# Edge feature projections moved from the attention stage into stage one

## The reference

```python
q = (xn @ Wq + bq).reshape(n, H, DH)     # n = 2500, H = 8 heads, DH = 32
k = (xn @ Wk + bk).reshape(n, H, DH)
v = (xn @ Wv + bv).reshape(n, H, DH)
ep = ef @ We + be                        # ef: 40000 x 64, We: 64 x 32
scores = jnp.einsum('ehd,ehd->eh', q[dst], k[src] + ep[:, None, :]) * scale
scores = scores * ew[:, None]
m = segment_max(scores, dst); ex = jnp.exp(scores - m[dst])
attn = ex / segment_sum(ex, dst)[dst]
out = segment_sum(attn[:, :, None] * v[src], dst) @ Wo + bo
```

## Time and profile before

| | us |
|---|---|
| median of 3 runs (1723.24 to 1728.3) | 1725.58 |
| span of the profiled execution, first to last instruction | 1668.6 |
| median above that span | 57.0 |
| PE busy with matmuls | 1495.7 |
| DVE busy | 1028.6 |
| POOL busy | 781.2 |
| ACT busy | 615.6 |

### The profile page before, as it was taken

One profiled execution on the slowest core, in us unless ns is written; L12 is line 12 of the kernel. 1 busy time (PEld: TensorE's weight loads), 2 busy tenths in 40 slices (PEclk: granted clock), 3 DMA queues, 4 the chain that ended last, 5 costly groups with the idle time before them and its releaser, 6 DMA issues. The chain is left out here.

```text
span 1668.6 us, 23723 instructions
## 1 busy us (share of the span) xinstructions
PE 1495.7 (90%) x6795; PEld 1005.9 (60%) x6795; DVE 1028.6 (62%) x2542; ACT 615.6 (37%) x1534; POOL 781.2 (47%) x738
## 2 busy tenths in 40 slices
PE   4999788999999999998356799999999999999996
PEld 2554314665666777777233467767766767767785
DVE  6543244345445555545388789898898888896432
ACT  3121002333234343443022355554555445555341
POOL 1100277646755777600378666574746556540000
PEclk9999857999999999999556699999999999999997
DMA  8448456546766566631487885665757565641100
GB/s 258 164 161 261 142 151 172 154 115 191 213 175 180 166 190 178 164 94 47 137 252 216 267 253 165 193 180 167 208 152 212 143 196 169 179 122 39 29 7 9
DMA packets 191573, 270.07 MB, mean 162 GB/s; under 512 B 28295, under 2 KB 156035, under 8 KB 188867
## 3 DMA queue, kind: packets, MB, share of 16 engines
q1 hardware_dynamic: 148419, 144.77, 27.7%
q0 software_dynamic: 43008, 123.61, 26.8%
HBM read 196.22 MB, written 72.06 MB: 161 GB/s over the span
## 5 line engine op out<-in xcount | busy, mean ns | idle before, releaser
L1890 POOL DMA_INDIRECT att_kv<-table_kv,g_srcI x314 | 368.5, 1174 | 246.4 <-issue 180.4
L1149 POOL DMA_INDIRECT ex_hg<-table_h,z_idx x314 | 316.7, 1008 | 150.2 <-issue 84.9
L2441 PE MATMUL att_psR<-g_mw,att_h 128*128 128x256 f32 x640 | 163.9, 403 | 1.0 <-ACT att_h L2259 1.0
L2414 PE MATMUL att_psR<-att_t,g_mw 128*128 128x256 f32 (+1 forms) x640 | 154.8, 387 | 0.1
L1466 PE MATMUL ex_psG<-ex_hg,ex_oh 128*42 128x256 f32 x628 | 134.6, 427 | 13.3 <-DMA ex_hg<-table_h,z_idx 7.2
L751 PE MATMUL tab_psH<-e_u,tab_xT 128*128 128x512 f32 x320 | 142.6, 598 | 4.3 <-DVE e_u L532 4.3
L2441 PEld LDWEIGHTS att_psR<-g_mw,att_h 128*128 128x128 f32 x640 | 124.7, 200 | 23.0 <-ACT att_h L2259 4.0
L1387 ACT ACTIVATE ex_h<-ex_psH,g_cols 128x256 f32<-128x256 f32 (+1 forms) x240 | 97.3, 464 | 93.8 <-PE ex_psH L1488 93.1
L2414 PEld LDWEIGHTS att_psR<-att_t,g_mw 128*128 128x128 f32 x640 | 121.2, 199 | 16.6 <-issue 2.6
L1882 POOL DMA_DIRECT2D table_o<-att_part x59 | 54.2, 919 | 161.9 <-DMA table_o<-att_part 90.5
L2301 PE MATMUL att_psG<-att_kv,att_oh 128*42 128x264 f32 x628 | 109.5, 431 | 13.7 <-DVE att_kv L1997 13.3
(11 more groups left out here) (308 smaller groups left out, 2465.1 us busy)
## 6 DMA issues: line engine op xcount, KB each, us to landing
table_h<-tab_hs SPq DMA_DIRECT2D x20, 1024.0 KB, 4.0
att_eft<-in_eft SPq DMA_DIRECT2D x158, 64.0 KB
ex_db<-table_dst SPq DMA_DIRECT2D x79, 126.0 KB
table_ohT<-ex_ohT SPq DMA_DIRECT2D x79, 126.0 KB
att_ohT<-table_ohT SPq DMA_DIRECT2D x79, 126.0 KB
table_oh<-ex_oh SPq DMA_DIRECT2D x79, 84.0 KB, 2.3
att_oh<-table_oh SPq DMA_DIRECT2D x79, 84.0 KB, 4.0
table_kv<-ex_qkv SPq DMA_DIRECT2D x10, 512.0 KB, 4.8
```

The costliest lines, as they stand in the source:

```text
L1149: nc.gpsimd.indirect_dma_start(hg[:, t % RING0, :], None, d.h[:, :], bass.IndirectOffsetOnAxis(ap=g.idx0[:, t:t + 1], axis=0)).then_inc(go ...
L1890: nc.gpsimd.indirect_dma_start(kv[:, t % (RINGC * TP), H:H + 2 * D], None, d.kv[:, :], bass.IndirectOffsetOnAxis(ap=g.srcI[:, t:t + 1], ax ...
L2414: ins = nc.tensor.matmul(out[:, c * CB:c * CB + used(b)], g.mw1[:, e, k, c * P:(c + 1) * P], t3[:, k, 0:used(b)], start=(k == 0), stop=(k ...
L2441: ins = nc.tensor.matmul(out[:, q * D:(q + 1) * D], h1[:, n % 3, k, q * P:(q + 1) * P], g.mw2[:, e, k, :], start=(k == 0), stop=(k == DK - 1))
```

## The change

The projection leaves the attention stage and is made in stage one, in `NEC = 20` chunks of four groups (`EC = 4`; the last has three). For each chunk SP loads the features (two DMAs, 256 KB in all for a full chunk), PE makes eight products of the old size into one bank of `psH`, ACT copies 128x512 values to one of three buffers `epK`, and SP stores them (`keep`, 256 KB) to a new table `table_ep` in memory. Twelve chunks stand early, at places 2.3, 3.9, ... 19.9 of PE's order, and eight late, at 91.2, 91.7, ... 94.7. Feature buffers: six, four of them in the not yet used space of the feed-forward weights for the early chunks and in the gather ring for the late ones. The loads of those feed-forward weights wait until the early chunks are made. In the attention stage one load for four groups brings the result straight into `epb`. SP's program, doubled for two forms of the inputs, is now doubled in stage one and single in the attention stage.

```diff
+EC = 4
+NEC = -(-NG // EC)
+EIN, EOUT = 6, 3
+def place_ep(c):
+    return EP_AT + EP_PACE * c if c < NEARLY else EP_LATE + EP_LATE_PACE * (c - NEARLY)
+EP_AT, EP_PACE = 2.3, 1.6
+NEARLY, EP_LATE, EP_LATE_PACE = 12, 91.2, 0.5
 def order0(groups, engine):
     out = []
+    if groups and engine in ("PE", "ACT"):
+        out += [(place_ep(c), "ep", c, 0) for c in range(NEC)]
+    if groups and engine == "SP":
+        out += [(place_ep(c - EIN + 1) + 0.5 if c >= EIN else EP_AT + 0.9 * (c - 4), "eft", c, 0) for c in range(2, NEARLY)]
+        out += [(place_ep(c - EIN) + 0.2 if c >= NEARLY + EIN else NG + 1.5 + 0.01 * c, "eft", c, 0) for c in range(NEARLY, NEC)]
+        out += [(place_ep(c) + (1.2 if c < NEARLY else 0.3), "keep", c, 0) for c in range(NEC)]
...
+                        if what == "ep":
+                            n = min(EC, NG - EC * b) * P
+                            act.wait_ge(s.half_made, half["ep", b, 0] + 1)
+                            if b >= EOUT:
+                                act.wait_ge(ep_stored[b % EOUT], 16 * (b // EOUT))
+                            nc.scalar.copy(epK[:, b % EOUT, 0:n], psH[:, half["ep", b, 0] % 3, 0:n]).then_inc(s.half_ready, DK)
...
+                def features(c):
+                    if c == 0:
+                        pe.wait_ge(s.we_loaded, 32)
+                    n = half["ep", c, 0]
+                    pe.wait_ge(eft_got[eft_at(c)], 32 * eft_round(c))
+                    if n >= 3:
+                        pe.wait_ge(s.half_ready, DK * (n - 2))
+                    for i in range(min(EC, NG - EC * c)):
+                        out = psH[:, n % 3, i * P:(i + 1) * P].rearrange("p (a t c) -> p a t c", a=2, c=DH)
+                        for t in range(2):
+                            ins = nc.tensor.matmul(out[:, :, t, :], eft_chunk(c)[:, i, t * P:(t + 1) * P], g.we[:, :], start=True, stop=True)
+                    ins.then_inc(s.half_made, 1)
...
+                def load_features(c, features):
+                    if c == NEARLY:
+                        sp.wait_ge(s.summed, NG)
+                    if c >= NEARLY + EIN or EIN <= c < NEARLY:
+                        sp.wait_ge(s.half_made, half["ep", c - EIN, 0] + 1)
+                    elif c >= NEARLY:
+                        sp.wait_ge(s.half_made, half["ep", NEARLY - 1, 0] + 1)
...
+                def keep_features(c):
+                    n = min(EC, NG - EC * c) * P
+                    sp.wait_ge(s.half_ready, DK * half["ep", c, 0] + DK)
+                    sp.dma_start(d.ep[c * P:(c + 1) * P, 0:n], epK[:, c % EOUT, 0:n]).then_inc(ep_stored[c % EOUT], 16)
...
 SLOT1 = {
-    "PE": (("sums", -0.271), ("feat", -0.236), ("cols", -0.027), ("turnS", 0.247), ("carry", 0.444), ("turnR", 0.580), ("ends", 0.830), ("ques", 0.900)),
+    "PE": (("sums", -0.271), ("cols", -0.027), ("turnS", 0.247), ("carry", 0.444), ("turnR", 0.580), ("ends", 0.830), ("ques", 0.900)),
...
-    "ACT": (("odd", -0.123), ("exp", 0.044), ("pw", 0.245), ("feat", 0.502), ("scale", 1.507)),
+    "ACT": (("odd", -0.123), ("exp", 0.044), ("pw", 0.245), ("scale", 1.507)),
...
-                    dve.wait_ge(s.ep_ready, i + 1)
+                    dve.wait_ge(ep_got[i // EC % 2], 16 * (i // EC // 2 + 1))
...
-                def load_features(i, features):
-                    if i >= INS:
-                        sp.wait_ge(s.ep_made, i - INS + 1)
-                    for a in range(2):
...
+                def load_features(c):
+                    if c >= 2:
+                        sp.wait_ge(s.added, EC * (c - 1))
+                    n = min(EC, NG - EC * c)
+                    sp.dma_start(epb[:, c % 2, 0:n, :, :].rearrange("p i t c -> p (i t c)"), d.ep[c * P:(c + 1) * P, 0:n * P]).then_inc(ep_got[c % 2], 16)
...
-                        if what == "loadE" and b + INS < NG:
-                            load_features(b + INS, features)
+                        if what == "loadE" and b % EC == 0 and b // EC + 1 < NEC:
+                            load_features(b // EC + 1)
```

More of the change, by code:

```diff
@@ L1106, in stage_sums_experts @@
         for what, b, e in orders["PE"]:
-            if what in ("A", "B"):
+            if what in ("A", "B", "ep"):
                 half[what, b, e] = len(half)
-        assert [v for v in orders["PE"] if v[0] in ("A", "B")] == [v for v in orders["ACT"] if v[0] in ("A", "B")]
+        assert [v for v in orders["PE"] if v[0] in ("A", "B", "ep")] == [v for v in orders["ACT"] if v[0] in ("A", "B", "ep")]
         before, last = {}, None
@@ L1125, in pair, with eft_chunk, eft_at, eft_round @@
             return (2 * i, 2 * i + 1) if 0 <= 2 * i < NSG else ()
+        def eft_chunk(c):
+            j = eft_at(c)
+            if j >= 4:
+                return eftN[:, j - 4, :, :]
+            if c >= NEARLY:
+                return hg[:, j * EC:(j + 1) * EC, :]
+            return f_rings[j // 2][:, j % 2 * EC:j % 2 * EC + EC, :]
+        def eft_at(c):
+            return (c if c < NEARLY else c - NEARLY) % EIN
+        def eft_round(c):
+            return len([n for n in range(c + 1) if eft_at(n) == eft_at(c)])
         def spots_of(i):
@@ L1641, in program @@
                             load_nodes(i)
+                        for to in (g.we[0:ED, 0:DH], g.we[ED:P, DH:2 * DH]):
+                            sp.dma_start(to, d.we).then_inc(s.we_loaded, 16)
+                        for c in range(2):
+                            load_features(c, features)
                     for what, b, e in orders["SP"]:
+                        if what == "eft":
+                            load_features(b, features)
+                        if what == "keep":
+                            keep_features(b)
                         if what == "store":
@@ L1690, in program @@
                         sp.wait_ge(s.grp_stored, 16 * len(CH))
+                        for j, sem in enumerate(ep_stored):
+                            sp.wait_ge(sem, 16 * len(range(j, NEC, EOUT)))
                         sp.wait_ge(s.later, 64)
-                program(sp)
+                if redo:
+                    program(None)
+                else:
+                    with sp.If(sp.value_load(g.flags[0:1, 1:2], min_val=0, max_val=1)):
+                        program(d.eft)
+                    with sp.If(sp.value_load(g.flags[0:1, 0:1], min_val=0, max_val=1)):
+                        program(d.efs)
         m.clear()
@@ L1803, in stage_attention @@
         in_got = [m.cleared_sem(f"in_got{b}") for b in range(INS)]
-        eft_got = [m.cleared_sem(f"eft_got{b}") for b in range(INS)]
+        ep_got = [m.cleared_sem(f"ep_got{b}") for b in range(2)]
         oh_got = [m.cleared_sem(f"oh_got{b}") for b in range(3)]
@@ L2277, in queries @@
                     ins.then_inc(s.q_ready, 1)
-                def features(i):
-                    pe.wait_ge(eft_got[i % INS], 32 * (i // INS + 1))
-                    if i >= 1:
-                        pe.wait_ge(s.ep_ready, i)
-                    for c in range(TP // 2):
-                        ins = nc.tensor.matmul(psE[:, c * 2 * DH:(c + 1) * 2 * DH], eft[:, i % INS, c * P:(c + 1) * P], g.we[:, :],
-                                               start=True, stop=True)
-                    ins.then_inc(s.ep_made, 1)
                 def sums(i):
@@ L2531, in steps @@
                     sp.wait_ge(s.out_stored, 16 * NC)
[L2533 to L2539 removed]
+                steps()
         m.clear()
```

65 lines of the change are left out of this document (24 added, 41 removed).

## The result

The changed kernel took 1732.19 us (median of 20 runs), the kernel before 1720.16 (20 runs beside them): a ratio of 1.0075, 95% interval 1.0051 to 1.0099, so about 13 us slower. I had forecast no change, 1723.3. The time lies inside my range, but the forecast was wrong. Every ratio in this text is the one on record, taken from the fast runs of both kernels, and can differ by up to 0.2% from the quotient of the two medians.

The account below looks back on a forecast made before the run. PE was taken to bound stage one and the attention stage, with DVE close behind in the latter. Stage one +24.7 and attention -27 gave -2.3 us, so 1723.3 us; range 1708 to 1738.

Parts of the forecast that it names:

- twelve early and middle chunks: Stage one, chunks 0 to 11: early six +7.5 us (bounds +2 and +15), middle six +11.8 us.
- late eight: Border of the stages, chunks 12 to 19: +5.4 us net, part hidden in PE's idle time; bounds +4 and +7.
- attention, groups 0 to 24: Attention stage before 960 us: removed edge feature products give back 3 us, between 0 and 8.
- groups 24 to 78 and the tail: Attention stage, 960 to 1500 us: of 28.4 us of PE work removed, 24 us comes through.
- Early chunks: Stage one ahead of block 0's turn, chunks 0 to 5: 2 + 3 + 3.8 - 1.3 = +7.5 us.
- the hold of SP that I priced at 3 us: Ahead of block 0: chunk 4's store on SP holds up group 8's store, +2.3 to +4.2 us, taken as +3.
- The rule of the Trainium skill: Early stretch: sustained activity releases the clock throttle, which would make the early term about +2 instead of +7.5 us.
- what keeps it under 28.4 is VectorE: Attention stage: VectorE, at 470.67 of about 512 us, and POOL's ring keep the gain at 24 us.
- Another bound takes over: Rival, attention stage: only half of 28.4 us comes through, +8.5 us, 1734 us; chance 0.16.
- POOL's ring: Attention stage, in that rival: gathers wait for the sum nine groups back, so shorter slots make VectorE wait more.
- The sign I had listed: Attention stage: PE idle time growing by more than 10 us, with waits on DVE or gathers, would show the forecast wrong.
- 57 us: Whole kernel: runs' median of 1725.58 us over the profiled span of 1668.6, taken as unchanged launch and surrounding time.

Follow-up runs that it names:

- e8: Changed kernel with all twelve early and middle chunks placed behind the start of block 0, nothing left out: 1740.02 us, ratio 1.0104.
- e9: Changed kernel with only the store of chunk 4 moved behind that of group 8 in SP's order: 1738.32 us, ratio 1.008.
- e10: Changed kernel with filler of 12 and 2 unneeded matmuls at each block's gate, traced; the timed runs of this kernel: 1741.5 us, ratio 1.0079.
- e11: Changed kernel with VectorE's edge feature addition cut to the first of eight heads: 1712.03 us, ratio 0.9925.
- e13: Changed kernel with filler matmuls per block, seven ahead of the gate and one ahead of the turned gate: 1714.26 us, ratio 0.9944.
- e15: Changed kernel with chunk 3 moved to place 6.95 and the store of chunk 4 behind that of group 8: 1731.4 us, ratio 1.0064.
- e16: Changed kernel with chunk 3 and chunk 4's store moved, and filler of seven and one, shortened in blocks 0, 7 and 8: 1718.84 us, ratio 0.9955.
- e1: Kernel before, no edit, traced a second time: 1725.45 us, span 1724.0.
- e6: Kernel before with filler matmuls per block, five ahead of the gate and two ahead of the turned gate: 1717.42 us, ratio 0.9969.
- e12: Kernel before with VectorE's edge feature addition cut to the first of eight heads: 1724.23 us, ratio 1.0016.
- e14: Kernel before with filler matmuls per block, three ahead of the gate and one ahead of the turned gate: 1712.6 us, ratio 0.9941.
- e17: Kernel before, unchanged, traced a third time: 1725.01 us, span 1723.5.
- e18: Kernel before with filler of three and one per block, repeated on the same chip as the changed kernel with filler: 1716.23 us, ratio 0.9929.
- e2: Changed kernel without any chunks, the attention stage reading its features from the k/v table: 1715.79 us, ratio 0.9943.
- e3: Changed kernel with only the late chunks 12 to 19 made, the rest read from the k/v table: 1727.7 us, ratio 0.998.
- e4: Changed kernel with the early chunks' feature loads spread, each placed 0.15 of a group ahead of its chunk: 1779.83 us, ratio 1.0293.
- e7: Changed kernel without chunks 0 to 5, only 6 to 19 made: 1722.81 us, ratio 0.9994.

## Why the prediction was wrong, point by point

The terms against the means of traces with the same stage. Stage one: eight traces with all chunks (changed, e8, e9, e10, e11, e13, e15, e16) against six without (e1, e6, e12, e14, e17, e18). Attention stage: eight traces of the change's code without filler (changed, e2, e3, e4, e7, e8, e9, e15) against e1 and e17. The tail is the time from group 78 to the end of the span.

| term | forecast, us | measured, us | from |
|---|---|---|---|
| twelve early and middle chunks | +19.3 | +17.2 | ScalarE's hidden layer of block 9's router at 803.0 against 785.8 |
| late eight | +5.4 | +9.1 | first product with queries at 891.3 against 865.0, less the line above |
| attention, groups 0 to 24 | -3 | -1.1 | 177.2 against 178.3 |
| groups 24 to 78 and the tail | -24 | -12.4 | 500.3 against 508.8, 167.1 against 171.0 |
| sum | -2.3 | +12.8 | runs: 1720.16 x 0.0075 = +12.9 |

- **Stage one** came out near in sum, 26.3 for 24.7, but partly by luck, since 3.5 us of it is a pause that no term of mine had (next point). The twelve early and middle chunks cost 1.4 us each, where my two terms come to 1.6. A middle chunk took PE 1.89 us, close to the 1.96 of the price. That less than this came through fits a PE that is not as full between 290 and 820 us as the earlier trace rows made it: busy 503.78 to 507.94 of 530 in the two traces of before, 511.06 with the chunks. The late chunks took PE 14 us (838.11 to about 852), where I had 15.2, but gave back less at the border: the first projection took 4.51 us, where I had counted on 2.7. From the last `C` of block 9 to the end of its last projection it is 23.6 us with the chunks and 16.9 without, so +6.7 for my +5.4.

The border in the changed kernel, the chunks 12 to 19, the turn, the two projections:

```profile
838.11 7.25 PE L1522 MATMUL ex_psH<-g_we,ex_hg 128*128 128x64 f32 x64
845.20 3.74 PE L1522 MATMUL ex_psH<-g_we,ex_eft 128*128 128x64 f32 x32
848.78 3.29 PE L1522 MATMUL ex_psH<-g_we,ex_hg 128*128 128x64 f32 x28
851.90 0.61 PE L365 MATMUL ex_psW<-g_ident,ex_xn 128*128 128x128 f32 x4
855.03 4.51 PE L1571 MATMUL ex_psW<-z_wqkv,ex_x2T 128*128 128x512 f32 x8 [2.52 <-ACT ex_x2T L1474]
859.38 2.74 PE L1571 MATMUL ex_psH<-z_wqkv,ex_x2T 128*128 128x512 f32 x8
```

- **The pause behind it.** SP's doubled program ends with a second read of the flag and a jump over the other copy, while all engines wait for SP. The change moved the doubling from the attention stage to stage one, and the pause with it. The end of stage one on SP and the first gather of the attention stage, in the changed kernel:

```profile
867.51 0.49 SPq L1758 DMA_DIRECT2D table_u<-e_u  x1
L1782 SPq TENSOR_LOAD <-g_flags x1: 442/442/442, 870.3 to 870.3; - x1
L1782 SPq COMPARE_BRANCH  x1: 50/50/50, 871.1 to 871.1; - x1
876.16 1.08 POOL L1978 DMA_INDIRECT att_kv<-table_kv,g_srcI  x1 [104.90 <-issue]
```

  And before (e17), without the second read:

```profile
850.26 0.50 SPq L1675 DMA_DIRECT2D table_u<-e_u  x1
855.53 1.08 POOL L1890 DMA_INDIRECT att_kv<-table_kv,g_srcI  x1 [93.09 <-issue]
```

  From the last projection to the first gather it is 14.0 to 14.3 us in twelve traces with the change's code, e2 without a single chunk among them, and 10.6 or 10.7 in the seven traces without it. The last stretch gives the same back: from VectorE's last instruction to the end it is 8.2 us in the mean of the eight traces, 11.8 before. So 3.5 of the +9.1 are no cost of the chunks, and 3.7 of the -12.4 are no gain from the products.
- **Early chunks**: the hold of SP that I priced at 3 us came through the store of chunk 3, one group earlier than I looked, and block 0's turn came 12 to 13 us later where I had some 9. Taking 5 or 6 us of it back was worth nothing that the runs can tell (e8, e15). The loads were no cost that the runs show. The rule of the Trainium skill that activity releases the clock ("TensorE: Matmul & The Clock Gate", The HAM clock gate) did not pay for them: the changed kernel shows 0.65 in 232 to 250 us, but so does e17 without a chunk (0.64), and with PE just as busy, 17.66 of 18 us, e9, e13 and e16 show 0.50 there.
- **Attention, the step that failed.** I took 24 of 28.4 us, since PE was 96% busy and the chain gave its products 3.9%. The step "what keeps it under 28.4 is VectorE" named the right engine and sized it at 4 us, and the sum had no term for a longer wait at the gate and the clock behind it. Of the 26.5 us between groups 24 and 78, 8.5 came through. With the clock held (e13 and e16 against e14 and e18, which has one fall of 3.4 us) it is 486.3 against 502.2, so 15.9. With VectorE relieved it is 25.9. Taken on to VectorE's last instruction, which leaves out SP's pause, the three are 8.7, 17.3 and 26.7. So about 7 to 9 us went to the clock and about 10 to VectorE's side, as far as the one pair with the short addition can say. The 3 us at the start of the stage were mostly not there; their upper bound should also have been 10 and not 8, by the figures that I gave.
- **Rivals.** "Another bound takes over" was the case that came, at not far from its price (+8.5 for +12.8), but not by its mechanism, so the price was luck. POOL's ring did not tighten: its waits for the sums in this stretch went from 62.5 to 53.5 us. What came were VectorE's chain to the gate and the clock behind the wait. I had given the case 0.16. The sign I had listed was PE idle time with waits on DVE. At the gate it grew from 8.0 to 17.9 us, though PE's whole idle time in the stretch grew by 6 us only (28.3 to 34.5), under the 10 I had named. That each wait would also halve the clock for what follows I had not priced.
- **The base.** I added 57 us as time that lies around the span, with no row for it. A single trace that differs from the median by 3% of the kernel is a trace of another pattern: PE was idle for 16.6 us between groups 24 and 78 there, and for 28.3 and 30.0 in the other two, so the stage looked more bound by PE than it commonly is.

## What to carry to other kernels

Work taken from the engine that binds a stage is worth its full time only where the next engine doesn't stand right behind: look for the one wait per block at which PE meets VectorE, and count what it becomes. In this kernel a wait that grew cost twice, once itself and once by the clock of the work behind it; a few matmuls of the length of the wait, into a bank that is overwritten anyway, held the clock, and a few too many cost all that they brought. Look also at what moves along with the work: a program doubled at another place carried a pause of 3.5 us to it. Compare a profiled execution with the timed runs before building a sum on it.

## What the runs showed of the hardware

- Three matmuls of filler and one more, in ten places, made the kernel before 0.6 to 0.7% faster (e14, e18). PE's waits of 1.33 and 0.54 us, one shortly behind the other, were followed by a clock of 0.50 at 10 of 18 gates in the three traces of the unchanged kernel, and the changed kernel's waits of 2.7 to 3.1 and 0.54 us at all six of its gates. The Trainium skill ("TensorE: Matmul & The Clock Gate", HAM oscillation) tells of a kernel in which every wait for data is followed by work at the low clock; the changed kernel's gates show the same.
- With VectorE's addition cut, POOL's gather instructions took 992 ns each and not 1188 (e12 against e17, 209 rows each), and 1054 and not 1182 in e11 against the changed kernel. In e17 the 61 gathers that run beside this addition took 1.47 us each in the mean, the other 148 took 1.07. The Trainium skill ("SBUF — State Buffer", Terms) has VectorE and GpSimd share one pair of ports, the loser waiting; these rows agree, but do not show the port. So e11 relieves POOL as well as VectorE, and the 10 us put down to VectorE's side are not shown to be VectorE's alone.
- A second read of a flag and a jump at the end of SP's program held all engines for some 3.5 us: 14.0 to 14.3 us from the last projection to the first gather with it, 10.6 without.
